# Order of the last four tiles' ternary rows, and who normalises the first three routing tiles

## The reference, cut to what matters

```
x = x + tanh(g_xattn[0]) * L0_xattn(layernorm(x), ctx, mask, ...)   # 16 heads of 32, softmax
x = x + tanh(g_ffn[0])   * L0_ffn(layernorm(x), weight, bias)       # ternary weights, 8 bit rows
x = x + tanh(g_xattn[1]) * L1_xattn(layernorm(x), ctx, ctx)         # sigmoid scores, no heads
x = x + tanh(g_ffn[1])   * L1_ffn(layernorm(x), gate_w, ...)        # 16 experts, top 4, 2 shared
```

```
x_scale = max(abs(xn)) / 127                 # L0_ffn, one scale for each row
x_q = clip(round(xn / x_scale), -127, 127)
out = (x_q @ w_ternary.T) * gamma * x_scale + bias
...
score = sigmoid(einsum('bdn,bdm->bnm', Q, K) / sqrt(128))   # L1_xattn: 512 x 512 for each tile
out = einsum('bvn,bnm->bvm', V, score)
```

## Time and profile before

| | us |
|---|---|
| median of 3 runs | 1305.1 |
| lowest, highest | 1303.42, 1305.77 |
| the profiled execution | 1304.01 |
| its span in the trace | 1302.3 |

### The profile page before, as it was taken

One profiled execution on the slowest core, in us unless ns is written; L12 is line 12 of the kernel. 1 busy time (PEld: TensorE's weight loads), 2 busy tenths in 40 slices (PEclk: granted clock), 3 DMA queues, 4 the chain that ended last, 5 costly groups with the idle time before them and its releaser, 6 DMA issues. The chain is left out here.

```text
span 1302.3 us, 25685 instructions
## 1 busy us (share of the span) xinstructions
PE 1219.5 (94%) x7835; PEld 1027.9 (79%) x7836; DVE 666.7 (51%) x1407; ACT 577.8 (44%) x1387; POOL 431.6 (33%) x518
## 2 busy tenths in 40 slices
PE   6998999999999789979999999999999999999995
PEld 6876788788787567756777787889999889998995
DVE  6556555555545699833666654642233553424241
ACT  4555356356356568864111111543344553434342
POOL 1102211210213375440004761334434344343433
PEclk9999999999999789979999999999999999999998
DMA  9100000000000013023000231865446656645454
GB/s 331 37 17 20 17 1 20 18 1 18 17 18 9 10 33 108 9 91 115 1 1 1 68 131 49 255 148 102 76 81 141 181 143 158 146 81 135 85 139 72
DMA packets 54335, 100.36 MB, mean 77 GB/s; under 512 B 5094, under 2 KB 21990, under 8 KB 54262
## 3 DMA queue, kind: packets, MB, share of 16 engines
q0 software_dynamic: 15824, 37.76, 15.4%
q1 hardware_dynamic: 38438, 61.65, 14.5%
HBM read 72.91 MB, written 26.48 MB: 76 GB/s over the span
## 5 line engine op out<-in xcount | busy, mean ns | idle before, releaser
L1871 PE MATMUL t_H<-m_W,t_xT 128*128 128x352 f32 x1632 | 280.3, 327 | 6.8 <-DVE m_W L1949 5.2
L1871 PEld LDWEIGHTS t_H<-m_W,t_xT 128*128 128x128 f32 x1632 | 261.7, 188 | 9.7 <-DVE m_W L1949 7.6
L1839 POOL DMA_INDIRECT out_dram<-t_ys,t_sid x68 | 109.8, 1615 | 220.4 <-ACT t_ys L1900 109.2
L1916 ACT ACTIVATE t_sl<-t_H 128x352 f32<-128x352 f32 x68 | 31.5, 463 | 174.1 <-PE t_H L1871 174.1
L722 ACT ACTIVATE pr<-SC,neg 128x128 f32<-128x128 f32 x256 | 89.9, 377 | 39.3 <-DVE neg L927 39.3
L46 PE MATMUL t_Y<-m_W,t_hT 128*128 128x512 f32 (+1 forms) x207 | 87.4, 422 | 5.0 <-issue 3.1
L1994 DVE TENSOR_TENSOR t_hT<-t_TH,t_hT 128x384 fp32r<-128x384 f32 x68 | 37.9, 557 | 101.8 <-ACT t_hT L1937 100.6
L1900 ACT ACTIVATE t_ys<-t_Y,t_wcol 128x512 f32<-128x512 f32 x69 | 47.3, 686 | 93.2 <-PE t_Y L48 93.2
L1970 DVE TENSOR_TENSOR t_h<-t_H,t_sl 128x352 f32<-128x352 f32 x68 | 35.6, 523 | 103.5 <-ACT t_sl L1916 103.5
L48 PE MATMUL t_Y<-m_W,t_hT 128*128 128x512 f32 (+1 forms) x207 | 81.8, 395 | 0.0
L47 PE MATMUL t_Y<-m_W,t_hT 128*128 128x512 f32 (+1 forms) x207 | 81.4, 393 | 0.0
(11 more groups left out here) (473 smaller groups left out, 3230.7 us busy)
## 6 DMA issues: line engine op xcount, KB each, us to landing
m_raw<-in_L_ffn_w_dram SPq DMA_DIRECT2D x28, 704.0 KB, 5.8
m_raw<-in_L_ffn_w_dram SPq DMA_DIRECT2D x14, 512.0 KB, 6.7
rows_d<-before_w SPq DMA_DIRECT2D x17, 256.0 KB, 2.0
CT<-in_ctx_dram SPq DMA_DIRECT2D x8, 512.0 KB, 3.8
X<-in_x_dram SPq DMA_DIRECT2D x4, 1024.0 KB, 13.0
out_dram<-X SPq DMA_DIRECT2D x3, 1024.0 KB, 4.3
m_raw<-in_L_ffn_w_dram SPq DMA_DIRECT2D x14, 192.0 KB, 7.1
CT<-in_ctx_dram SPq DMA_DIRECT2D x8, 256.0 KB, 2.8
```

The costliest lines, as they stand in the source:

```text
L1839: pool.indirect_dma_start(out=m["out_rows"][:, :], out_offset=bass.IndirectOffsetOnAxis(ap=sid[:, b:b + 1], axis=0), in_=ys[:, b, :], in_o ...
L1871: x_ = pe.matmul(bk[b % 2][:, 0:I], xT[:, b % 2, jx, k, :], W13[:, jw, k, j, :], start=k == 0 and jx == jw, stop=k == KC - 1 and jx == 1)
```

## The change: what it does

Three parts.

1. The end of the last group's text. Before, the two context transposes `aT.0`, `aT.1` and the ternary rows of tiles 12 and 13 (`u`, `uT`, `fm`) stand between the last heads' steps. Now the heads' steps stand closer together, `ra.0` stands behind the last two `sm`, and `rc.3`, `bc.3`, `on.3`, `oT.3` stand ahead; `ag.0.0` and `ag.0.1` come behind `oT.3`.
2. `between`. `u`, `uT` and `fm` of tiles 12 and 13 are now among the first eight score tiles, and those of tiles 14 and 15 stand later than before: `u.14` ahead of score tile 12 (before 7), `u.15` 16 (10), `uT.15` 21 (13), `fm.14` 18 (12), `fm.15` 24 (16). `ta.1`, `tb.1`, `tc.1` and those of number 2 move as well.
3. Routing. DVE, not ACT, normalises the first three tiles (`ROWS_DVE`), then makes `fold`, then `row_scale`; ACT begins with the first weight split, and its other splits stand after tiles 1, 4 and 5 (before: 0, 2, 5 and 6).

```
-            "bc.2 pv.5 on.2 oT.2 st.1 pT.12 v.3 ra.0 Sa.7 pT.13 Sb.7 sm.14 sm.15 "
-            "oP.2 aT.0 rb.0 pv.6 aT.1 rd.0 u.0 pT.14 uT.0 aS.0.0 u.1 pT.15 aS.0.1 rc.3 fm.0 ag.0.0 bc.3 pv.7 uT.1 ag.0.1 on.3 oT.3 "
-            "aS.0.2 fm.1 oP.3 ", NG - 1)
-        between = {0: "sf.-4", 1: "st.-2", 2: "sf.-3", 3: "st.-1", 5: "ra.-1", 6: "rb.-1", 7: "rd.-1 u.-2", 9: "uT.-2", 10: "u.-1",
-                   12: "fm.-2", 13: "uT.-1", 16: "fm.-1", 18: "sf.-2", 20: "sf.-1", 22: "ta.1", 24: "tb.1", 26: "tc.1", 28: "sw", 36: "ta.2", 40: "tb.2",
-                   42: "tc.2", 52: "ta.3", 56: "tb.3", 58: "tc.3"}
+            "bc.2 pv.5 on.2 oT.2 st.1 pT.12 v.3 Sa.7 pT.13 Sb.7 sm.14 sm.15 ra.0 "
+            "oP.2 rb.0 pv.6 pT.14 rc.3 aS.0.0 pT.15 rd.0 bc.3 aT.0 pv.7 on.3 oT.3 aS.0.1 ag.0.0 aT.1 ag.0.1 "
+            "oP.3 aS.0.2 ", NG - 1)
+        between = {0: "u.-4", 2: "uT.-4", 3: "u.-3 fm.-4", 4: "st.-2", 5: "uT.-3", 6: "st.-1 sf.-4", 7: "fm.-3", 8: "ra.-1", 10: "rb.-1 sf.-3",
+                   12: "rd.-1 u.-2", 14: "uT.-2", 16: "u.-1",
+                   18: "fm.-2", 21: "uT.-1", 24: "fm.-1", 26: "sf.-2", 28: "sw", 29: "sf.-1", 32: "ta.1", 34: "tb.1", 36: "tc.1",
+                   44: "ta.2", 48: "tb.2", 50: "tc.2", 52: "ta.3", 56: "tb.3", 58: "tc.3"}
...
-        FIRST_SPLIT_AT = (0, 2, 5, 6)
+        FIRST_SPLIT_AT = (1, 4, 5)
+        ROWS_DVE = 3
...
-                for t in range(3):
-                    norm(t)
+                split_hi(0, 0)
...
+                    if t == 0:
+                        act.wait_ge(normed, ROWS_DVE)
                     if t + 3 < NB:
                         norm(t + 3)
                     if t in FIRST_SPLIT_AT:
-                        split_hi(0, FIRST_SPLIT_AT.index(t))
+                        split_hi(0, 1 + FIRST_SPLIT_AT.index(t))
...
+                for t in range(ROWS_DVE):
+                    dve.tensor_scalar(xn[:, t, :], X[:, t, :], c["rstd"][:, t:t + 1], c["mean"][:, t:t + 1], ALU.mult, ALU.add)\
+                        .then_inc(normed, 1)
+                dve.tensor_tensor(fold, c["identF"][0:2 * E, 0:E], c["identF"][0:2 * E, E:2 * E], ALU.add).then_inc(g_lo, 1)
                 row_scale(dve, c, scales, slice(3 * GB, NB), 1e-5)
```

More of the change, by code:

```diff
@@ L1676, in _ @@
                         dve.wait_ge(g_hi, 1)
-                        dve.tensor_tensor(fold, c["identF"][0:2 * E, 0:E], c["identF"][0:2 * E, E:2 * E], ALU.add).then_inc(g_lo, 1)
                         dve.tensor_tensor(gwT[:, :, 1, :], G.rearrange("p (k e) -> p k e", k=KC),
```

## The result

The changed kernel takes **1305.7 us** (median of 20 runs, 1303.6 to 1312.1); the kernel before, on the same chip, 1303.4 us (20 runs, 1300.7 to 1306.7). The ratio is **1.0033, interval 1.0023 to 1.0043**: slower by 0.33%, where 5 us less were forecast.

A forecast was written before the change was run, and what follows sets the result against it. TensorE, busy 1219.5 of 1302.3 us, was taken as the bound, so time is won only where it waits or runs at low clock. Gains of 4.5 (score tiles) and 0.5 (routing) gave 1305.1 - 5.0 = 1300.1 us, range 1294 to 1307.

The forecast's parts named there:

- The ledger of before: Heads' end and score tiles: 14.9 us idle plus 7.8 at half clock, 22.7 lost; 19.4 after, gain 3.3.
- Part 1: End of the heads: `bc.3` at 424.0 instead of 434.64 us, `oP.3` near 429.0 instead of 441.29.
- The list of waits in part 2: TensorE's waits in the heads' end and score tiles: 15.2 us in all, as much as before, none over 2.7.
- The placing of the steps in part 2: Score tiles: 0, 3 and 8 read out near 443, 473 and 508 us; gain 4.8 us, taken as 4.5.
- Part 3: Routing: DVE norms, earlier `fold`, no split between tiles 6 and 7; gain 0.5 us, bounds 0 and 1.5.
- The hold that I put on L94: Routing: `row_scale`'s L94 waits for POOL's 3.18 us operation; first gate product at 567.4 as before, otherwise 1.0 us earlier.
- POOL's queue holds TensorE: `ks.2`, `ks.3`, `ks.6` behind `fm` additions: POOL needs 6.3 us, waits 3.6 to 4.6; 1308.5 us, chance 0.16.
- its point of decision: Score tiles: POOL time, addition of `fm` to end of `ks`, of some 5.5 us, from which the slower case decides.
- The rival of a dense handover: Score tiles: the 1.9 and 2.7 us waits fall to about 1, clock stays 2.4 GHz; 1293 us, chance 0.12.
- The rival of DVE and POOL paying it back: `u.13` to `u.15` meet `ks`, 4.8 us instead of 2.4; 1304 to 1306 us, chance 0.22 together with only routing.
- the signs that I had named: Trace: `bc.3`, `oP.3`, tiles 0, 3, 8 times; 5 to 7 us on L445; L804 about 2; low clock twice.
- the three signs of being wrong: Tile 3 read out after 478 us, one `ks` wait over 3.5 us, or low clock for more than 15 us.

The follow-up runs named there:

- e4: Changed kernel with the `fm` steps of tiles 12, 13 and 14 moved from score tiles 3, 7, 18 to 4, 8, 20 (`sf.12` too): 1297.4 us, ratio 0.9966.
- e6: e4 with POOL's routing power (L109) moved ahead of its first two weight splits: 1295.5 us, ratio 0.9939.
- e7: Changed kernel with only tile 14's `fm` step moved, from score tile 18 to 20: 1305.5 us, ratio 1.0014.
- e5: Changed kernel with POOL's routing power (L109) moved ahead of its first two weight splits: 1304.2 us, ratio 1.0010.
- e10: Changed kernel with POOL's routing power (L109) moved between its first and second weight splits: 1305.6 us, ratio 1.0029.
- e12: Changed kernel with ACT making its first two weight splits in a row, so POOL's second follows its first directly: 1310.6 us, ratio 1.0061.
- e1: The changed kernel itself, unedited, run again beside the kernel before: 1309.6 us, ratio 1.0045.
- e2: Changed kernel with the routing of the kernel before, keeping the new order of heads and score tiles: 1304.7 us, ratio 1.0017.
- e9: Changed kernel with only the `fm` steps of tiles 12 and 13 moved, to score tiles 4 and 8 (`sf.12` too): 1298.7 us, ratio 0.9981.
- e8: e4 with the routing of the kernel before: 1296.9 us, ratio 0.9950.

## Why the prediction was wrong

- **The ledger of before** (14.9 us idle, 7.8 at half clock) held as a bound: by tile 8, e4 and e6 took 7.3 us of it.
- **Part 1 was right.** `bc.3` at 424.13 (forecast 424.0) behind 1.00 us of wait (1.0), `oP.3` at 429.36 (429.0) behind 1.65 (1.9).
- **The list of waits in part 2 was right.** Forecast 0.8, 2.7, 1.7, 2.7, 1.9 and 1.4 us for `u.12`, `ap.1.0`, `ks.2`, `ks.3`, `ks.6` and `u.14`; measured 0.86, 2.29, 1.56, 2.97, 2.42 and 1.51. The clock fell twice, as forecast, from 444 to 451 and from 485 to 489 us, the second behind `ks.6` instead of `ks.3`.
- **The placing of the steps in part 2 is the step that failed**, and I had taken its figure: 4.5 us of gain, measured 0.4 at tile 8. The ledger beside it said 3.3. Tile 3 was read out 5.7 us ahead, not 7. Then "of these go `fm.15` (0.7 us), and `sf.14`, `sf.15` and `ta.1` ... 1.5 us" leaves out the wait for `ks.6`, which my own list had at 1.9 us, and the low clock that came with it. From tile 3 to tile 8 the changed kernel takes 38.0 us; with `fm.14` alone moved (e7) it takes 35.3, which is what I had placed (473 to 508). That wait with its half clock is 2.7 us. 32.8 us of the kernel before were the comparison: there tiles 4 to 8 are dense, so nothing was to be won behind tile 3, and every wait there is a plain loss.
- **Part 3**: 0.5 us of gain, measured 0.2 us of loss in the lower group (12.49 against 12.30 us from tile 15 to the gate). The hold that I put on L94 fell on L91, with the same effect; what the split removed between tiles 6 and 7 was worth, no run shows by itself (from the gate to the experts the traces before and after differ by 0.3 us, with the clock low in different places). What I did not see at all was **POOL's second split**. I laid the row scale beside the first and never asked where the second would fall: 0.32 us behind it in one trace, 0.15 us ahead in another. It costs 3 us by itself, and only kernels that it can reach have runs above 1308 (the changed one, e7 and e12; none of the 19 runs of e5 and e10). These runs pull the median up.
- **The rival "POOL's queue holds TensorE"** (1308.5) named the right queue and the right direction. From the addition to the end of `ks` POOL took 5.2, 4.8 and 5.7 us, only the last above its point of decision (5.5), and the waits were 1.6, 3.0 and 2.4 us instead of 3.6 to 4.6. The rival of a dense handover (1293) failed on the same three waits; e6 comes near it with 1295.5, with the routing's power moved as well. The rival of DVE and POOL paying it back had the nearest number (1304 to 1306) and the wrong mechanism: `u.13` and `u.14` took 2.4 and 2.7 us, not 4.8. Some rests of `ag` (L854) did take 1.7 instead of 0.7 us, but no wait that the view puts to them is over 0.3 us.
- **The sum as measured**, profiled execution, against the trace before: 0.5 us ahead when the experts start instead of 5.0; then 0.8 us lost at half clock in the last nine matmuls and 0.6 among the experts: 0.9 behind, which is the lower group. The upper group makes it 0.33% in the ratio.

Of the signs that I had named, `bc.3`, tiles 0 and 3, the sum for L445 and the fall of L804 came true; tile 8 at 508 did not (512.1), and it was the one on which the gain hung. None of the three signs of being wrong came: tile 3 was read out at 474, the longest wait for `ks` was 3.0 us, and the clock was low for some 10 us. They could not see a loss behind tile 3 or in the routing.

**What stays open**: why the upper group lies 3 us further up than the catch accounts for, and which of its runs have it (one of them was profiled). The rest goes with the clock. In e12, with the catch in every run, the two runs at 1306.7 and 1306.9 us have a mean granted clock of 0.980 and 0.981, and the four above 1310 have 0.976. The kernel before does the same without a catch: of its 29 runs beside e1 to e4, the eight at 0.983 took 1300.0 to 1301.2 us, the sixteen at 0.979 or less 1302.0 to 1306.4. The two traces of the changed kernel lie 9.7 us apart from the common row to the end: 2.9 us are the catch, and the rest fell where the clock was low. 2.4 us were lost in the score tiles (e1_again's first stretch of half clock lasted 10 us instead of 7, and it had a second one, 459 to 463), 1.5 us between the gate and the end of the routing, where the clock was low three times, 1.5 us in the experts' first 24 products (5.66 against 4.11 us) and 1.1 us in the last nine. e2 lost 1.7 us in its score tiles in the same way, without a catch, and its runs show one group. What makes the clock fall in one execution and not in the next is not shown.

That a clock standing high at the routing's start lets ACT's second split come early is argued from four traces: with first transposes of 1.97, 1.77, 1.38 and 1.11 us (after, e9, e1, e7) POOL's second split came 0.32 and 0.12 us behind the start of L97, then 0.15 and 0.13 us ahead of it. I could not set the clock and so have not tried it.

## What to carry to other kernels

Place a handed-out step behind the queue entry that the critical engine needs next, not ahead of it: the same three additions, one score tile or two later, were worth 7 us. When times are worked out by placing steps, check at the end that every wait of the list is also in the placing. And when a small operation is moved beside another engine's long ones, look at every one of them, and at the margin: 0.3 us of slack beside a hold of 3 us, and the kernel has runs with it and runs without it.

## What the runs showed of the hardware

- A 128x4 operation on VectorE waited out a whole POOL operation of 3.16 us that had begun 0.03 us ahead of it (L91), and a `tensor_scalar` of 128x4 did so too (L97, 3.03 us). In every such row here (also L93 in e12 and L103 in e5) POOL's operation had begun first; with the power ahead of the splits, L91 to L97 took 0.15 to 0.17 us each.
- The granted clock at one and the same place differs between executions of one kernel: 0.83 and 0.74 from 440 to 460 us in two executions of the changed kernel. Behind waits of 2.3 to 3.0 us it fell in all traces of the new order, though not behind each of them; with none over 1.8 us it stayed at 1.00 in the score tiles of e4 and e6 and fell once, from 462 to 466 us, in those of e8, behind a wait of 1.83 us. Behind the 3.0 us ahead of the last nine matmuls it was low in ten traces and not in those of before, e4, e10 and e12.
- The same kernel can have two groups of run times 6 us apart on one core. A collision decided by 0.3 us makes 3 us of it; the rest goes with the granted clock, 0.978 to 0.983 in the lower group of the first 20 runs and 0.974 to 0.977 in the upper.
